# Attention's first tiles: VectorE's key padding and maxima ahead of the norm operations, input statistics four tiles per body, the second tile normalised first

## The reference

```python
ln_out = layernorm(hidden_states, ln1_s, ln1_b)     # over 256 channels, eps 1e-5
q, k, v = jnp.split(ln_out @ w_qkv + b_qkv, 3, axis=-1)
scores = einsum('bhqd,bhkd->bhqk', q, k) / sqrt(16) # 16 heads of 16 channels
scores = scores * mask - 10000.0 * (1.0 - mask)
ctx = einsum('bhqk,bhkd->bhqd', softmax(scores), v)
x = hidden_states + ctx @ w_ao + b_ao
# then: cross attention with the context, an MLP of 1024, and the recurrent block
```

## Time and profile before

| | us |
|---|---|
| median of 3 runs | 1112.36 (1111.42 to 1115.19) |
| the profiled execution | 1112.93 |
| its span in the trace | 1111.1 |

### The profile page before, as it was taken

How to read it: one execution, slowest core, us unless ns; L and a number is a source line. 1 busy time by engine, 2 the same in 40 slices (tenths; PEclk the granted TensorE clock), 3 DMA queues, 4 the chain that set the end, 5 groups by cost and what they waited for, 6 DMA issues and landing times.

```text
span 1111.1 us, 34641 instructions
## 1 busy us (share of the span) xinstructions
PE 1054.2 (95%) x12992; PEld 880.4 (79%) x12992; DVE 889.2 (80%) x1532; ACT 767.4 (69%) x1910; POOL 607.4 (55%) x535
## 2 busy tenths in 40 slices
PE   5899999999999998999999999999999999887888
PEld 4789899888899887777787787788787787666677
DVE  5987777888777776127999999999999999999643
ACT  4778778777777775566666766666776667744774
POOL 4777887877878875024433444443444443453332
PEclk9999999999999998999999999999999999999999
DMA  8500000011111110003333321333321233304011
GB/s 325 181 4 1 0 0 2 3 41 41 46 43 38 42 44 2 1 14 82 77 86 86 86 59 40 73 85 85 85 68 39 64 86 86 86 17 107 20 38 58
DMA packets 39868, 65.01 MB, mean 59 GB/s; under 512 B 4384, under 2 KB 26208, under 8 KB 39392
## 3 DMA queue, kind: packets, MB, share of 16 engines
q1 hardware_dynamic: 39776, 63.75, 21.5%
HBM read 55.35 MB, written 8.39 MB: 57 GB/s over the span
## 4 chain that ended last, share of the span: by engine, by line
PE 84%; DVE 8%; issue 4%; ACT 3%; POOL 1%; DMA 0%; ACTq 0%; DVEq 0%; POOLq 0%
PE psum L1010 10%; PE psum L1001 10%; PE psum L353 9%; PE psum L1091 9%; PE psum L267 6%; PE psum L336 5%; PE psum L368 5%; PE psum L297 4%; PE psum L280 3%; PE psum L1050 3%; PE psum L1130 2%; PE psum L1163 2%; PE psum L310 2%; PE psum L1272 2%; DVE shared L1832 2%
## 5 line engine op out<-in xcount | busy, mean ns | idle before, releaser
L1832 DVE TENSOR_TENSOR_SCAN shared<-late_wT,shared 128x512 f32<-128x512 f32 x128 | 194.0, 1516 | 0.0
L232 POOL TENSOR_TENSOR shared<-shared,att_row_max 128x512 f32<-128x512 f32 x128 | 132.4, 1054 | 16.9 <-DVE att_row_max L564 16.9
L453 ACT ACTIVATE shared<-shared 128x512 f32<-128x512 f32 x128 | 80.4, 631 | 69.7 <-POOL shared L232 69.6
L353 PE MATMUL psum<-shared 128*128 128x128 f32 x1024 | 126.0, 276 | 1.0 <-ACT shared L462 1.0
L1001 PE MATMUL psum<-late_glnT,w 128*128 128x256 f32 x512 | 119.8, 387 | 1.8 <-ACT late_glnT L1380 1.8
L353 PEld LDWEIGHTS psum<-shared 128*128 128x128 f32 x1024 | 120.2, 193 | 1.4 <-ACT shared L462 1.4
L1010 PE MATMUL psum<-w,late_hT 128*128 128x256 f32 x512 | 120.0, 383 | 1.3 <-ACT late_hT L1389 1.2
L564 DVE TENSOR_REDUCE att_row_max<-shared 128x8 f32<-128x512 f32 x128 | 86.9, 680 | 40.9 <-POOL shared L225 40.9
L896 POOL TENSOR_TENSOR late_xm<-late_mixed,late_xa 128x512 f32<-128x512 f32 x64 | 78.0, 1228 | 72.6 <-DVE late_mixed L1798 72.6
L1001 PEld LDWEIGHTS psum<-late_glnT,w 128*128 128x128 f32 x512 | 95.9, 192 | 18.0 <-issue 2.8
L905 POOL TENSOR_TENSOR shared<-shared,late_rT 128x512 f32<-128x512 f32 x32 | 40.7, 1270 | 122.9 <-DVE shared L1832 122.9
(11 more groups left out here) (169 smaller groups left out, 2474.6 us busy)
## 6 DMA issues: line engine op xcount, KB each, us to landing
shared<-v_rows SPq DMA_DIRECT2D x64, 512.0 KB, 7.6
shared<-in_enc SPq DMA_DIRECT2D x64, 128.0 KB, 2.6
v_rows<-shared SPq DMA_DIRECT2D x64, 64.0 KB, 1.8
out<-x SPq DMA_DIRECT2D x16, 256.0 KB, 2.0
x<-in_x SPq DMA_DIRECT2D x7, 512.0 KB, 9.8
w<-in_w SPq DMA_DIRECT2D x2, 1024.0 KB, 17.0
shared<-in_cross_mask SPq DMA_DIRECT2D x1, 1024.0 KB, 11.4
shared<-in_w_qkv SPq DMA_DIRECT2D x1, 768.0 KB, 4.7
```

Source lines behind the costliest of these rows:

```text
L232: nc.gpsimd.tensor_tensor(zs, zs, peak.unsqueeze(2).to_broadcast([P, PAIRS, S]), ALU.subtract).then_inc(shifted, 1)
L353: last = nc.tensor.matmul(dst[:, half * P:(half + 1) * P], w[:, kb, c0 + half * P:c0 + (half + 1) * P], src[:, u % 2, kb, 0:P], start=(kb ...
L453: nc.scalar.activation(probs[:, u % 2, half * 4:(half + 1) * 4, :].rearrange("p r k -> p (r k)"), z[:, u % 2, half, :], ACT.Exp).then_inc( ...
L1832: nc.vector.tensor_tensor_scan(states, wT[:, u, half, :, :, :].rearrange("p j b t -> p (j b t)"), states, 0.0, ALU.mult, ALU.add).then_inc ...
```

## The change

Four things change, all at the start of self attention. The number of instructions on each engine stays the same.

1. ScalarE normalises tile 1 before it copies tile 0's transposed values (body -5), not after.
2. VectorE in the filling bodies pads the keys and finds the maxima directly behind the mask (and `shifts`), ahead of `spreads` and `variances` and of all input statistics but those of part 2.
3. The input statistics of parts 3 to 8 stand at the end of VectorE's body, behind key padding and maxima, in all bodies. They come one part (four tiles) per body, from body -2 to body 3; before, body -1 had two parts and the last came in body 2.
4. The `spreads` of group 4 (tiles 12 to 31) move from body 3 to body 4, where its `variances` were already.

```diff
-    STATS_AT = {2: -3, 3: -2, 4: -1, 5: -1, 6: 0, 7: 1, 8: 2}
-    NORM_AT = {1: -5, 2: -3, 3: 0, 4: 3, 5: TILES - 8, 6: TILES, 7: ALL - 6}
-    VAR_AT = {i: n + int(i > 2) for i, n in NORM_AT.items()}
+    STATS_AT = {2: -3, 3: -2, 4: -1, 5: 0, 6: 1, 7: 2, 8: 3}
+    NORM_AT = {1: -5, 2: -3, 3: 0, 4: 4, 5: TILES - 8, 6: TILES, 7: ALL - 6}
+    FIRST_STATS = 2
+    VAR_AT = {i: n + int(i == 3 or i > 4) for i, n in NORM_AT.items()}
...
@@ scalar_part, body
                 copy_probs(*on(k, t, 1))
+            first = not looped(t) and k * TILES + t == -5
+            if first:
+                normalise(*on(k, t, 6), u + 6)
             if there(*on(k, t, 5)):
                 copy_ln(*on(k, t, 5), u + 5)
...
-            if there(*on(k, t, 6)):
+            if there(*on(k, t, 6)) and not first:
                 normalise(*on(k, t, 6), u + 6)
...
@@ vector_part, body
             for i in NORM_AT:
                 if n_is(n, VAR_AT[i] + 1):
                     shifts(i)
-            for i in STATS_AT:
-                if n_is(n, STATS_AT[i]):
-                    load_stats(i)
+            filling = not looped(t) and n < 0
+            if n_is(n, STATS_AT[FIRST_STATS]):
+                load_stats(FIRST_STATS)
+            if there(*on(k, t, 4)) and filling:
+                pad_keys(*on(k, t, 4))
+            if there(*on(k, t, 3)) and filling:
+                find_max(*on(k, t, 3), u + 3, 0)
+                find_max(*on(k, t, 3), u + 3, 1)
             for i in NORM_AT:
                 if n_is(n, NORM_AT[i]):
                     spreads(i)
                 if n_is(n, VAR_AT[i]):
                     variances(i)
-            filling = not looped(t) and k * TILES + t < 0
-            if there(*on(k, t, 4)) and filling:
-                pad_keys(*on(k, t, 4))
-            if there(*on(k, t, 3)):
+            if there(*on(k, t, 3)) and not filling:
                 find_max(*on(k, t, 3), u + 3, 0)
             if there(*on(k, t, 4)) and not filling:
                 pad_keys(*on(k, t, 4))
-            if there(*on(k, t, 3)):
+            if there(*on(k, t, 3)) and not filling:
                 find_max(*on(k, t, 3), u + 3, 1)
+            for i in STATS_AT:
+                if i > FIRST_STATS and n_is(n, STATS_AT[i]):
+                    load_stats(i)
```

More of the change, by code:

```diff
@@ L517, in stats_by @@
                 return starts[1]
-            loaded = max([1] + [j for j in STATS_AT if STATS_AT[j] <= NORM_AT[i]])
+            loaded = max([1] + [j for j in STATS_AT if STATS_AT[j] < NORM_AT[i] or j == FIRST_STATS and i >= j])
             return starts[loaded + 1] + max(0, NORM_AT[i])
```

## The result

| | before | after |
|---|---|---|
| median in one comparison, 15 runs each | 1115.19 us (1111.42 to 1138.34) | 1118.29 us (1116.59 to 1119.86) |
| ratio | | 1.0034 [1.0023, 1.0045] |
| the profiled execution | 1112.93 us | 1119.63 us |
| its span | 1111.1 us | 1117.9 us |
| mean granted clock of TensorE in it | 0.992 | 0.984 |

The change makes the kernel slower by 0.34%, or 3.8 us. (That is the ratio of the means, 1118.34 to 1114.57, without the one disturbed execution of 1138 us; between the two medians lie 3.1 us.) The forecast was 1114.2 us (1110.4 to 1117.0), with most of the chance on "no change". The time lies outside the range. Part of this is the base: the three runs shown for before had a median of 1112.36 us, fifteen have 1115.19, which is 2.8 us more and the larger part of the 4.1 us by which the median was missed.

What follows compares the result with a forecast made beforehand. VectorE was taken to bound bodies 0 to 5 and TensorE the loop after; lag terms 1.33 - 0.07 + 0.03 + 0.49 gave +1.8 us at mask 8, so 1112.4 + 1.8 = 1114.2 us, range 1110.4 to 1117.0.

Steps and rivals of the forecast that it cites:

- the open assumption: Body -3: GpSimd's short residual-bias add also blocks a norm operation; mask 1 at 22.5 us, without blocking 21.95.
- mask 1: Body -3: norm operations beside a busy GpSimd delay this mask from 22.05 to 22.5 us, lag +0.45.
- body 0: Mask 3 to mask 4: statistics now behind the last maximum; 8.05 us instead of 8.03, lag +0.20.
- body 1: Mask 4 to mask 5: statistics delay the next mask directly; 8.12 us instead of 6.99, lag +1.33, the largest term.
- body 4: Spreads and variances together make this body 7.32 us instead of 6.83, +0.49.
- The lag at mask 8: Start of the TensorE-bound loop: mask 8 comes +1.8 us later than before, and this stays to the end.
- B: Rival: small norm operations slip through between GpSimd's halves in bodies -3, 0, 1 and 4; -2.2 us, 1110.2 us; chance 0.11.
- E: Rival: two of three VectorE shifts in bodies -2, 2, 5 meet both bias adds; +4.3 us, 1116.7 us; chance 0.11.
- D: Rival: early gain and late loss cancel, as with single stalls in bodies 1 and 4; +0.3 us, 1112.7 us; chance 0.17.
- C: Rival: GpSimd's subtraction and L215 do not block norm operations; -3.5 us, 1108.9 us; chance 0.03.
- The second tile first: Start of the fill: tile 1's transpose at 8.69 instead of 9.17 us, mask 0 at about 15.0, lag -0.5.
- Body -2: Late variances and a blocked shift put exps at 25.70 instead of 25.34 and score 2 at 27.64, lag +0.36.

Runs made afterwards that it cites:

- the changed order at full clock: Changed kernel plus dummy identity transposes on TensorE, 20 in body -2 and 8 each in bodies 1 and 2; 1114.68 us, ratio 1.0007 to before.
- the repeated pair: Both kernels run once more with nothing altered: before 1114.32 us, after 1118.31 us.

## Why the prediction was wrong

**What held.** The order of VectorE and its prices held. Norm operations stand still until a running GpSimd instruction ends, including L216 (0.65 us), which was the open assumption. Here the Trainium skill ("SBUF — State Buffer", section "Who interferes with whom") agrees with the trace: two-input VectorE operations are stopped (L534 for 1.01 us), and statistics and tensor_reduce are not (four statistics take 1.39 or 1.40 us wherever they stand, such as beside the subtraction at 26.66). Step by step: mask 1 at 22.71 (forecast 22.5), exps at 25.87 (25.70), body 0 7.91 (8.05), body 1 8.09 to 8.30 (8.12), body 2 without a clock fall 6.77 to 6.79 (6.76), body 4 7.36 (7.32). The statistics, 1.3 us long, cost 1.1 us in body 1 (8.09 against 6.99) because they left the shadow of the blocked operations. The lag at mask 8 was carried to the end (3.46 us, at L1791 3.5 us). Rivals B to E did not occur. B and D: the variances of body 1 were stopped twice (0.86 and 1.20 us), the spreads of body 4 too (0.89 and 1.30). C: L534 and L541 were stopped. E: the shifts behind masks 1, 5 and 8 took 0.85 to 0.88 us, a stop by one half, not by both. E's +4.3 us is the nearest to the measured difference, with a mechanism that did not occur.

**The second tile first, lag -0.5, was right on the mean and unseen in the pair.** It gives 0.40 us at the transpose; that mask 0 is 0.57 us earlier on the mean of six is partly luck, since single traces of one order differ by 0.8 to 1.1 us. What I took as given was that the projections behind it keep their length. They vary by 1.1 us between executions of any of these kernels, and the trace I worked from held a short one. From mask 0 on, my own steps give 71.7 - 15.0 = 56.7 us to mask 8, and the changed order at full clock takes 56.84. So the terms of the order were sized well: 2.4 - 0.4 = +2.0 us in the runs, +1.8 in the forecast.

**What failed: no step held TensorE's clock.** The step is "Body -2". My own times contained the wait: I had the scores of tile 1 ready by 20 and the exps, which the next transposes wait for, at 25.70, and between them TensorE has only 3.1 us of work (19.88 to 23.00 after). I priced the transposes behind the wait and score 2 at their old durations. The runs show them at half rate (1.12 and 1.16 instead of 0.71 and 0.69 us after), and the clock falls again in body 1 or 2, in the group behind a wait of 1.24 or 1.19 us for the residual add. In the fill this costs 0.9 us in one trace of the changed kernel and 2.2 us in the other, against the trace in which the engine was kept busy. The Trainium skill ("TensorE: Matmul & The Clock Gate", "Part 1: The HAM clock gate (the "warmup" mystery)") states that the low rate is the default and that activity releases it. The trace agrees: the first eight projections take 1.92 us at 9.27, and the same eight of the next tile 1.06 us at 15.69. The length of a wait alone does not say whether the clock falls: before keeps it behind an idle time of 2.60 us at 21.05, and the kernel with the statistics moved loses it behind 2.01 us at 21.28. I had looked at the clock in the steady loop alone, which has no gaps.

**And the base.** The forecast stood on 1112.4, the low end of what before does: its 15 runs have a median of 1115.19. With the difference right, the time would have been 1116.2: inside the range and still 2.1 us under the measured median. With the base right and the difference as forecast it would have been 1117.0. It took both errors to leave the range. The profiled execution of before had neither a long first group of projections nor a clock fall in the fill, and I took it as typical.

**The sum:** the order 2.4 us, the second tile -0.4 us, the clock 0.9 to 2.2 us, less 0 to 0.4 us that before loses in the same way, gives 2.5 to 4.2 us. Measured were 3.8 us [2.6 to 5.0].

**What stays open.** With the waits filled the time is 0.8 us above before [-1.1 to 2.6], so it recovers 3.0 of the 3.8 us, where the traces show 0.9 to 2.2 us in the fill. The rest has a place: in the profiled execution 3.7 us are gained between 434 and 461 us, where the clock stayed up. Whether the filled waits have any part in that, or chance alone, was not settled; nor were the falls near 1000 us in the first profile of the changed kernel. In the repeated pair nothing was gained or lost behind the fill.

## What to carry to other kernels

When a change makes an engine wait where it used to work, price the instructions behind the wait as well: for TensorE, look up in the profile how long the same group takes at its lower clock (here 1.16 against 0.69 us). Small operations that another engine's instructions stop are best put where that engine is idle, and work that is not stopped, such as statistics, belongs in the waits of the blocked chain; taking it out of there cost 1.1 of its 1.3 us. And take the base from more than one trace: two profiles of the same kernel had mask 8 1.2 us apart (before, 69.89 and 71.09) and 1.7 us (after, 73.35 and 75.09).

## What the hardware showed that I had not expected

- The six norm operations take 0.91 us beside an idle GpSimd and 2.72 us beside a busy one, though each handles only 4 elements per partition.
- The clock fell without any single long wait. Body 2 of the repeated changed kernel and of two experiments has such a fall. The two longest idle times of TensorE in the 20 us ahead of it were 1.03 and 1.19 us, 1.31 and 1.25 us, and 1.31 and 1.36 us. Whether it falls differs between executions of one kernel.
- The granted clock in the rows is not all that the duration depends on. Between 8 and 14 us it shows 1.00 after:

```profile
8.00:14.00 6.00, 5.18 (x26) 5.09 (x26) 2.58 (x11) 2.84 (x8) 0.00 (x0) 1.00 0.85 267
```

  Yet in that trace eight projections (L337) take 1.92 us at 9.27 and 1.06 us later on. The durations have to be read beside the column.
- TensorE paused for 0.69 and 0.75 us inside a group of equal matmuls when bulk loads ended, and for 0.59 to 1.31 us in six traces inside the projections at 35 to 39 us while they ran. It did not in the one trace in which those loads came later. Moving them gained 1.1 us in body 0.
